# Gated double delta-rule layer on one core: the end-decayed keys move from GpSimd to twelve ScalarE copies, and all five engines' work is written in a new order

## What is computed

```
kn = k / |k|                       # k, q, v, alpha, aR, beta, gamma: projections of the token
r  = clip(v - S^T kn, -1, 1)       # S's prediction error
S  = alpha * S;  S += beta  * kn (v - kn S)^T;   o  = S^T q
R  = aR * R;     R += gamma * kn (r - kn R)^T;   o += R^T q
out = o @ Wo^T + residual          # alpha, aR are vectors over the state's rows
```

## Time and profile before

| | before |
|---|---|
| median of 3 runs | 2472.81 us (2470.99 to 2474.99) |
| the profiled execution: its own time | 2473.48 us |
| its span, first to last instruction | 2471.7 us |
| mean granted TensorE clock | 0.974 of full speed |
| busy: TensorE matmul / weight load | 93% / 78% of the span |
| busy: VectorE, ScalarE, GpSimd | 71%, 43%, 52% |
| the chain that ended last | TensorE 59%, issue 20%, VectorE 14%, ScalarE 3%, DMA 2% |

### The profile page before, as it was taken

How to read it: one execution, slowest core, us unless ns; L and a number is a source line. 1 busy time by engine, 2 the same in 40 slices (tenths; PEclk the granted TensorE clock), 3 DMA queues, 4 the chain that set the end, 5 groups by cost and what they waited for, 6 DMA issues and landing times.

```text
span 2471.7 us, 119622 instructions
## 1 busy us (share of the span) xinstructions
PE 2299.7 (93%) x52544; PEld 1928.8 (78%) x52544; DVE 1754.5 (71%) x3725; ACT 1055.5 (43%) x1616; POOL 1286.6 (52%) x2440
## 2 busy tenths in 40 slices
PE   1999995799999999999999999999999999999997
PEld 1544543588888888888888888888888888888886
DVE  6101013688888878888888788888888888888884
ACT  2323222444444444444444444444444444444430
POOL 0000002656666656666666566666666666666661
PEclk8899997699999999999999999999999999999999
DMA  2000000111111121211111212111112122222221
GB/s 87 1 0 0 0 0 20 27 39 37 37 37 37 37 47 37 39 37 37 37 37 37 43 37 40 37 38 37 37 36 48 38 39 41 41 41 41 41 41 27
DMA packets 306089, 84.77 MB, mean 34 GB/s; under 512 B 280368, under 2 KB 302512, under 8 KB 305584
## 3 DMA queue, kind: packets, MB, share of 16 engines
q1 hardware_dynamic: 305584, 77.25, 15.6%
HBM read 41.53 MB, written 35.65 MB: 31 GB/s over the span
## 4 chain that ended last, share of the span: by engine, by line
PE 59%; issue 20%; DVE 14%; ACT 3%; DMA 2%; SPq 1%; POOL 1%; DVEq 0%; ACTq 0%; POOLq 0%
PE bank L454 10%; PE bank L434 3%; DVE Kt L823 3%; PE bank L416 3%; PE bank L405 3%; PE bank L489 3%; PE bank L498 3%; PE bank L396 3%; PE bank L411 3%; PE bank L613 3%; PE bank L423 2%; PE bank L580 2%; PE bank L399 2%; PE bank L531 2%; PE bank L522 2%
## 5 line engine op out<-in xcount | busy, mean ns | idle before, releaser
L1080 POOL TENSOR_TENSOR lane_t<-lane_n,lane_x 128x15 f32<-128x15 f32 (+7 forms) x960 | 326.7, 340 | 110.2 <-DMA lane_n<-n_dram 34.1
L1083 POOL TENSOR_TENSOR lane_x<-lane_x,lane_t 128x15 f32<-128x15 f32 (+7 forms) x960 | 340.5, 355 | 75.2
L454 PE MATMUL bank<-kq,Kt 64*64 64x96 f32 x8192 | 367.0, 233 | 7.1 <-issue 5.6
L454 PEld LDWEIGHTS bank<-kq,Kt 64*64 64x64 f32 x8192 | 315.2, 134 | 59.3 <-issue 58.9
L1032 POOL TENSOR_TENSOR dk<-cum 128x512 f32<-128x512 f32 x64 | 68.8, 1075 | 297.4 <-DVE cum L800 297.4
L1047 POOL TENSOR_TENSOR KQF<-efull,kn 128x768 f32<-128x768 f32 x64 | 119.5, 1867 | 161.1 <-ACT efull L1196 161.1
L1099 POOL MEMSET lane_id<- 128x256 f32 x1 | 0.3, 312 | 387.1 <-DVE acc L760 387.1
L757 DVE TENSOR_TENSOR dn<-bank,s3b 128x512 f32<-128x512 f32 x8 | 5.5, 692 | 239.5 <-PE bank L379 239.5
L1156 ACT ACTIVATE q<-bank 128x512 f32<-128x512 f32 x64 | 38.2, 597 | 317.3 <-PE bank L399 269.1
L1230 ACT ACTIVATE oS<-bank 128x512 f32<-128x512 f32 x64 | 38.2, 597 | 302.9 <-PE bank L602 302.9
L1165 ACT ACTIVATE ea<-bank,nba 128x256 f32<-128x256 f32 x256 | 107.5, 471 | 124.7 <-PE bank L405 103.3
(11 more groups left out here) (156 smaller groups left out, 6632.4 us busy)
## 6 DMA issues: line engine op xcount, KB each, us to landing
XF<-x_dram SPq DMA_DIRECT2D x256, 64.0 KB, 2.3
lane_n<-n_dram SPq DMA_DIRECT2D x128, 124.0 KB, 2.8
x_dram<-lane_x SPq DMA_DIRECT2D x128, 124.0 KB, 2.3
n_dram<-AS SPq DMA_DIRECT2D x256, 32.0 KB, 2.0
n_dram<-AR SPq DMA_DIRECT2D x256, 32.0 KB, 1.7
wt<-in_win SPq DMA_DIRECT2D x4, 640.0 KB, 4.6
out_y<-acc SPq DMA_DIRECT2D x16, 128.0 KB, 3.0
hw<-in_h1T SPq DMA_DIRECT2D x1, 1024.0 KB, 5.9
```

The source lines that it names most:

```text
L454: ins = pe.matmul(v3(dst[hd[h], o:o + kinds * C], kinds)[:, :, i * SUB:(i + 1) * SUB], Kt[hd[h], m * 96 + i * SUB:m * 96 + i * SUB + C], r ...
L1080: pool.tensor_tensor(tv, lane_n[:, m * SUB + m + 1:m * SUB + BASE].unsqueeze(2).to_broadcast([L, rows, m + 1]), xv[:, m, 0:m + 1].unsqueez ...
L1083: pool.tensor_tensor(xv[:, m + 1:, 0:m + 1], xv[:, m + 1:, 0:m + 1], tv, ALU.subtract).then_inc(s["lane_step"], 1)
```

## The change

`to_end` leaves GpSimd and becomes twelve ScalarE activations, each a copy of 64 columns scaled by one column of ek (a value for each partition). All bodies are rewritten in another order. VectorE and ScalarE push some steps one body later (`s_clip`, `r_right`, `r_solved` of chunk 3 and `add_out` belong to quad k-2, the masks to quad k+1, `log_decay` and `norms` on ScalarE to quad k+2), and each engine's loop gets one more body, which on TensorE is empty.

```
-            def to_end(n):
-                need(pool, "kdiag", n + 1)
...
+            def to_end(n):
+                need(act, "kdiag", n + 1)
+                need(act, "kfar", n + 1)
+                need(act, "kT_ps", 2 * n)
+                for m in range(4):
+                    for c in range(3):
+                        o = (m * NCH + c) * 96 + SUB
+                        ins = act.activation(kend[:, (m * 3 + c) * C:(m * 3 + c + 1) * C], Kt[:, o:o + C], ACT.Copy,
+                                             scale=ek[:, 6 * T + m * NCH + c:6 * T + m * NCH + c + 1])
+                ins.then_inc(s["kend"], 1)
```

SyncE's body, where `lanes_out` now comes after `lanes_in` of the same quad and ahead of the weight loads:

```
-                z, b, l, d, e = on(k + 4), on(k + 2), on(k + 1), on(k), on(k - 1)
-                if l:
-                    lanes_out(k + 1)
+                b = on(k + 2)
                 if b:
                     blocks_out(k + 2, 0)
                     blocks_out(k + 2, 1)
                     lanes_in(k + 2)
-                if z and (k + 4) % B == 0:
-                    load_weights(k + 4)
-                if d and (k) % B == 0:
-                    load_wo(k)
-                if e and k - 1 >= (QD - 1) * B:
+                    lanes_out(k + 2)
+                if on(k + 5) and (k + 5) % B == 0:
+                    load_weights(k + 5)
+                if on(k + 1) and (k + 1) % B == 0:
+                    load_wo(k + 1)
+                if on(k - 1) and k - 1 >= (QD - 1) * B:
                     store(k - 1)
```

GpSimd's body only loses `to_end`. One line of each other list:

```
@@ TensorE
                 if e:
-                    s_o(k - 1, 1)
-                    r_o(k - 1, 0)
...
+                    s_p(k - 1, 1)
+                    r_s(k - 1, 0)
@@ VectorE
-                a, b, d, e = on(k + 3), on(k + 2), on(k), on(k - 1)
+                a, b, l, d, e, f = on(k + 3), on(k + 2), on(k + 1), on(k), on(k - 1), on(k - 2)
@@ ScalarE
-            for k in range(-3, LAST + 2):
+            for k in range(-3, LAST + 3):
```

More of the change, by code:

```diff
@@ L626, in body @@
                 if e:
-                    r_s(k - 1, 1)
-                    s_p(k - 1, 2)
+                    s_w(k - 1, 2)
+                    r_w(k - 1, 1)
+                    s_o(k - 1, 1)
+                    s_y(k - 1, 2)
+                    r_y(k - 1, 1)
+                    r_o(k - 1, 0)
+                if a:
+                    project_kq(k + 3)
+                if e:
+                    s_s(k - 1, 2)
                 if d:
@@ L631, in body @@
                 if e:
-                    s_o(k - 1, 2)
-                    r_w(k - 1, 2)
-                    s_w(k - 1, 3)
+                    r_s(k - 1, 1)
+                if a:
+                    project_a(k + 3)
+                if e:
+                    s_p(k - 1, 2)
                 if d:
@@ L637, in body @@
                 if e:
+                    r_w(k - 1, 2)
+                    s_o(k - 1, 2)
+                if a:
+                    project_r(k + 3)
+                if e:
+                    s_w(k - 1, 3)
+                    r_o(k - 1, 1)
                     r_y(k - 1, 2)
                     s_y(k - 1, 3)
-                    r_o(k - 1, 1)
                 if a:
-                    project_kq(k + 3)
+                    norms(k + 3)
                 if d:
                     level1_nx(k)
-                if a:
-                    project_a(k + 3)
                 if e:
@@ L649, in body @@
                     s_p(k - 1, 3)
-                if a:
-                    project_r(k + 3)
                 if d:
                     level1_zd(k)
+                if a:
+                    project_v(k + 3)
                 if e:
+                    r_w(k - 1, 3)
                     s_o(k - 1, 3)
@@ L669, in body @@
                     products(k + 2, 2)
+                if e:
+                    r_o(k - 1, 2)
                 if d:
                     s_p(k, 0)
-                if e:
-                    r_y(k - 1, 3)
                 if b:
@@ L688, in body @@
                     s_o(k, 0)
-                    r_s(k, 0)
+                    s_y(k, 1)
+                if e:
+                    project_out(k - 1)
+                if d:
                     s_s(k, 1)
@@ L1244, in body @@
                     copy_kend(k + 1)
+                if b:
+                    to_anchor(k + 2)
                 if a:
                     copy_q(k + 3)
+                if d:
+                    level0(k)
+                if a:
                     gate(k + 3, 0)
                     squares(k + 3)
-                if d:
-                    level1(k)
-                if a:
                     gate(k + 3, 1)
-                    log_decay(k + 3, 0)
-                    log_decay(k + 3, 1)
-                if e:
-                    copy_out(k - 1)
-                if a:
-                    norms(k + 3)
-            for k in range(-3, LAST + 2):
+            for k in range(-3, LAST + 3):
                 body(k)
```

177 lines of the change are left out of this document (84 added, 93 removed).

## The result

| kernel | median us (lowest to highest) | executions |
|---|---|---|
| before | 2473.9 (2470.99 to 2477.96) | beside the changed one |
| changed | 2412.22 (2408.18 to 2413.72) | 4 |

The ratio is 0.9747, its 95% interval 0.9728 to 0.9766: faster by 2.5%, or 62 us. Forecast were 2419, with a range of 2393 to 2458.

The account below looks back on a forecast made before the run. TensorE, busy 290 of 300 us, sets the pace. A body saves 0.92 and gives back 0.05 + 0.1: 0.77 times 60 is 46 us, with 8 for weights 54; 2473.5 - 54 is about 2419, range 2393 to 2458.

Parts of the forecast that it names:

- three places of a body: TensorE's waits at r_y(2) for wR, project_r for ea, s_s(1) for yS: together 0.92 us a body.
- rival D: More goes: also half of the 0.5 between mean and undisturbed body, and the 0.15 given back: 2395 us; chance 0.09.
- 0.05 at `turn_kend`: TensorE's wait for the last kend copy, between on time and 0.15 us late; taken as 0.05 a body.
- 0.1 at `level1_zd`: TensorE's step after ScalarE's level1 copy, with only 0.75 us to cover it: 0.1 us late a body.
- (1) The copies: Twelve kend copies on ScalarE, each adding 0.22 us, 2.74 in all; kend there 4.8 to 5.1 after r_o(3).
- (2) wR: VectorE's wR no longer queues behind Kt, so the 0.47 us wait of r_y(2) on TensorE goes.
- (4) yS(1): TensorE's 0.25 us wait of s_s(1) for yS goes if VectorE scales AS in 0.73 us, as taken.
- (5) GpSimd: GpSimd loses 1.5 us a body, which it has spare; nothing gained there except through yS(1).
- (6) The weights: Reloads of wt ahead of a quad's first projection, three waits of 2.87 us: 8 us less, ends 0 and 12.
- Rival A: VectorE answers late in one or two places beside GpSimd, 0.53 us on from_anchors or scaling: 2449 us; chance 0.18.
- Rival B: Copies on ScalarE don't overlap, turn_kend waits 1.15 us a body: 66 us more, 2485 us; chance 0.09.

Follow-up runs that it names:

- e1: Changed kernel with to_end (kend) back on GpSimd as one multiplication, nothing of it on ScalarE: 2408.21 us.
- e12: Kernel before with kend's copies on ScalarE, the weight load earlier, and r_o(1) ahead of r_y(2) and s_y(3) on TensorE: 2427.55 us.
- e2: Kernel before, old order, with only kend's twelve copies moved from GpSimd to ScalarE: 2454.01 us.
- e8: Changed kernel plus one unused GpSimd multiplication released to run beside VectorE's scaling of AS: 2449.62 us.
- e4: Kernel before with only the weight load moved earlier on SyncE's queue, ahead of the second blocks_out and lanes_in: 2471.73 us.
- e7: Changed kernel with ScalarE making the kend copies ahead of vt and efull: 2487.7 us.
- e0: The changed kernel run again, on the chip of other follow-up runs: 2405.08 us.
- e3: Kernel before with only VectorE's own_half (Kt) moved behind r_right(2) and s_right(3): 2518.44 us.
- e9: Changed kernel plus one unused GpSimd multiplication directly behind far, beside VectorE operations that read PSUM: 2408.92 us.
- e10: Changed kernel with the lanes' and diagonal blocks' transfers cut short, so the inverses in the output are wrong: 2403.12 us.

## Why the prediction was right, point by point

The forecast of 2419 was 7 us high. The mechanism held: TensorE's waits in three places of a body and the weight loads. That the number came so close is in part luck, since errors of the terms offset each other: the undisturbed body gave 56 us where the sum had 46, the weights about 10 in the trace where it had 8, and the irregular loss of the other bodies, which the sum left as it was, grew by some 7 (rival D below).

- **The body.** The undisturbed body fell by 0.93 where the sum had 0.77. The 0.92 of the three waits is gone (from 1200 to 1500 us no row of TensorE's waits is left for wR, ea or yS). What the prediction gave back was 0.05 at `turn_kend`, measured as 0.08 (e1 against the changed kernel), and 0.1 at `level1_zd`, of which the waits show nothing. That makes 0.84; the other 0.09 is not assigned.
- **(1) The copies.** The place was right, the size a little low: twelve take 2.96, not 2.74, 0.239 from one to the next, not 0.22. That is the estimate worked out from the Trainium skill's figures (ScalarE: Activation LUTs, What ACT_TABLE_LOAD costs: 239 ns a copy and 2.96 in all); here the trace agrees. The 13 us more that it would have given did not come, since the hop from the last copy's end to `turn_kend` is 0.05 and not up to 0.24: kend was there at 5.02 to 5.07 after `r_o(3)`, where I had 4.8 to 5.1.
- **(2) wR.** Gone, as forecast. e12 took it away by itself and got 0.38 a body, in time 17 us instead of the 28 that 0.47 x 60 gives.
- **(4) yS(1).** Right and for the stated reason: the scaling of AS takes 0.71. From the end of `s_w(1)` (1313.42) to the end of yS(1) are 2.66 us, to `s_s(1)` 2.85, where the prediction had 2.6 and 2.8 (rows at the end of this section). e2 shows that GpSimd's kend multiplication was the cause in the old order, e8 that another multiplication in its place brings the wait back.
- **(5) GpSimd.** "Nothing gained there but (4)" is right; e1 goes further: in the new order the multiplication may stay on GpSimd and costs nothing that can be told, since the scaling of AS hardly ever starts in it (once in the 60 bodies; 0.79 in the mean of e1).
- **(6) The weights.** I took 8, from three times 2.87; the three waits were 2.9, 2.2 and 0.4, 5.5 us together, and went to 0.5. What brings the term back to about 10 in the trace of before is the lower clock behind the first two, 5 us, which the sum did not have: right in size by luck. e4 measured 6 for the move alone.
- **Rival A** named the right pair of engines, as a slowdown of 0.53. By the rows it is a wait for the rest of GpSimd's operation, and `from_anchors` escapes it, since it starts before GpSimd's (1.22 in the mean). A did not come since in this order the scaling of AS starts while GpSimd idles in nearly every body. e7 is A happening: one change of ScalarE's order, and the time is 14 us above the kernel before.
- **Rival B** has its price now: three copies more, 29 us. Its 66 us for a delay of 1.1 a body would have been too much by this measure (0.72 on the chain cost 0.48 in the mean).
- **Rival D** expected half of the 0.5 of irregular loss to go. 31.17 - 30.68 = 0.49 before, of which about 10 us / 60 = 0.17 are weights with their lower clock; 30.20 - 29.75 = 0.45 after (0.41 in e0), with 0.01 of weights. So without the weights it did not shrink but grew, from 0.32 to 0.44, some 7 us.

What I had wrong in the mechanism lay in the experiments: I moved Kt (e3) and the copies (e7) with the durations that the operations had in the old place. In the prediction the weights' price left out the clock, and 0.1 for `level1_zd` has no wait to show for it.

The rows for (4), VectorE and TensorE:

```profile
1315.80 0.28 DVE L918 TENSOR_TENSOR yS<-bank,betas 128x128 f32<-128x128 f32 x1
```

```profile
1316.27 0.45 PE L530 MATMUL bank<-yS,kendT 64*64 64x64 f32 x8
```

## What to carry to other kernels

When a step moves, take its duration from the place it goes to, not from the place it leaves: look what GpSimd is in at the moment the VectorE operation starts. If it has two SBUF operands, as all of those measured here, and a multiplication of GpSimd is under way, let it end 0.55 us (128x512) or 1.08 us (128x1024) after that one. The same instruction with two lengths in one trace (AS 1.26, AR 0.73) is the sign to look for. And where one engine is busy 97% of the time, the gain is the sum of its waits in one undisturbed body; price each of them, then check the new order for the one chain that everything queues behind.

## What the runs showed of the hardware

- A VectorE operation on two SBUF operands and a GpSimd one do not share time: the one that starts second ends late by about the rest of the first. In all 14 traces together, from 500 to 2300 us, 963 VectorE operations of 128x512 (the scalings and the halves of Kt) start inside a GpSimd `tensor_tensor` (other than the small inverses') that has more than 0.15 us left. 962 of them end 0.54 to 0.56 us after it, whether 0.16 or 1.59 us of it were left; the other one started 0.02 after it and kept its time. The 94 of 128x1024 end 1.08 to 1.09 after it. Alone they take 0.68 and 1.21. Those that VectorE started first kept 0.67 to 0.69 (585) and 1.21 to 1.22 (789).
- Examples: the scaling takes 1.26 in the mean beside kend (before), 1.58 beside 1.27 us of an unused multiplication (e8), 1.98 beside `against_state` (e7); a half of Kt 1.49 (before) and up to 1.79 (e3); 128x1024 with q 2.01 (e7).
- GpSimd loses in the same way when it comes second: the first multiplication of `against_state` takes 1.95 in the mean of the changed kernel, where `from_anchors` has 0.25 us left at its start, and 2.82 in the body of e8 shown, where it has 1.15 left and keeps its own 1.21. The second multiplication, of the same size, takes 1.82 with nothing of this kind beside it.

```profile
1298.72 2.82 POOL L1044 TENSOR_TENSOR KQF<-efull,kn 128x768 f32<-128x768 f32 x1 [0.54 <-ACT efull L1187]
```

- The Trainium skill (GPSIMD Engine Reference, Specifications) names the shared SBUF interfaces and the two-input condition. The runs agree: VectorE's masks out of PSUM kept their 0.59 beside the unused multiplication of e9.
- In the 60 bodies of the changed kernel TensorE has 30 stalls over 0.15 us with no releaser in the trace, at changing steps, of 0.17 to 1.24 us, 0.26 us a body; 0.20 in e0, 0.16 in the kernel before, 0.16 in e9 and 0.15 in e10, whose DMA share is 0.03 against 0.20 in e9.
- TensorE's weight waits of 2.9 and 2.2 us were followed by the lower level of its clock (before: granted clock 0.95 and 0.90 in these bodies). Without the waits (e4) it stayed at full speed.
